# First tokens of the projection: input in four transfers, and two pairs of products taken block by block with the weights' splitting

## The reference

```
x  = L0_attn_x                       # 4 x 1024 x 1024
xn = _layernorm(x, axis=-1)          # (x - mean) / sqrt(var + 1e-5)
q = (xn @ wq.T)                      # 1024 columns: 32 heads of 32
k = (xn @ wk.T)                      # 256 columns: 8 heads
v = (xn @ wv.T)                      # 256 columns
q, k = _apply_rope(q, cos, sin), _apply_rope(k, cos, sin)
...
y = softmax(q k / sqrt(32) + causal mask) v
s = y @ wo.T
g = silu(ffn(xn))                    # a small recurrence on the last token, a gate, a norm
out = x + s * g
```

## Time and profile before

| what | us |
|---|---|
| median of three runs (lowest, highest) | 2590.91 (2590.49, 2593.19) |
| the profiled execution | 2590.74 |
| its span | 2589.1 |
| TensorE busy in it | 2493.8 (96%) |
| VectorE, ACT, POOL busy | 1730.7, 980.8, 1368.0 |

### The profile page before, as it was taken

How to read it: one execution, slowest core, us unless ns; L and a number is a source line. 1 busy time by engine, 2 the same in 40 slices (tenths; PEclk the granted TensorE clock), 3 DMA queues, 4 the chain that set the end, 5 groups by cost and what they waited for, 6 DMA issues and landing times. The chain is left out here.

```text
span 2589.1 us, 43561 instructions
## 1 busy us (share of the span) xinstructions
PE 2493.8 (96%) x14180; PEld 1684.1 (65%) x14180; DVE 1730.7 (67%) x3500; ACT 980.8 (38%) x1645; POOL 1368.0 (53%) x637
## 2 busy tenths in 40 slices
PE   5999999996999999999999999999899999999998
PEld 4888888884555545554455545555378888888886
DVE  6444555444777777777777787777477777777777
ACT  2111111110666655666566656666431111111111
POOL 1122221122999989999899989999711111111111
PEclk9999999997999999999999999999999999999999
DMA  6544444537665665566466556555475666666666
GB/s 243 187 164 151 158 162 176 187 139 240 200 189 164 190 189 166 181 192 206 130 196 194 164 172 199 167 181 183 169 195 108 129 119 120 117 118 119 121 121 122
DMA packets 228017, 428.90 MB, mean 166 GB/s; under 512 B 16836, under 2 KB 99780, under 8 KB 227928
## 3 DMA queue, kind: packets, MB, share of 16 engines
q1 hardware_dynamic: 154536, 375.85, 43.7%
q0 software_dynamic: 73392, 51.91, 13.4%
HBM read 313.67 MB, written 113.51 MB: 165 GB/s over the span
## 5 line engine op out<-in xcount | busy, mean ns | idle before, releaser
L934 DVE CUSTOM_DVE_ANT_0 bcast<-mxp,mask_q 128x128 f32<-128x128 f32 (+7 forms) x1024 | 726.2, 753 | 307.1 <-PE mxp L1041 172.8
L855 ACT ACTIVATE pr<-stp 128x512 f32<-128x512 f32 x1152 | 649.5, 595 | 492.8 <-PE stp L1050 367.7
L1050 PE MATMUL stp<-qs,ks 97*128 97x512 f32 x1152 | 479.0, 454 | 3.5 <-ACT pr L855 2.7
L466 PE MATMUL eo<-xt,w 128*128 128x512 f32 x1920 | 448.8, 393 | 3.6 <-DVE xt L383 3.6
L804 POOL TENSOR_TENSOR acc<-acc,pr 128x2048 f32<-128x2048 f32 x96 | 440.8, 4592 | 4.4 <-POOL acc L804 3.8
L466 PEld LDWEIGHTS eo<-xt,w 128*128 128x128 f32 x1920 | 358.5, 189 | 77.2 <-issue 4.0
L1050 PEld LDWEIGHTS stp<-qs,ks 97*128 97x128 f32 x1152 | 209.4, 189 | 247.1 <-ACT pr L855 116.0
L1419 PE MATMUL gp<-g,xa 128*128 128x512 f32 x1536 | 357.1, 392 | 11.6 <-DVE g L1357 8.2
L1419 PE MATMUL op<-o,ya 128*128 128x512 f32 x1536 | 353.6, 390 | 0.8 <-DVE ya L1407 0.8
L1419 PEld LDWEIGHTS gp<-g,xa 128*128 128x128 f32 x1536 | 290.8, 189 | 72.8 <-DVE g L1357 8.5
L1419 PEld LDWEIGHTS op<-o,ya 128*128 128x128 f32 x1536 | 288.3, 188 | 61.3 <-DVE ya L1407 1.7
(11 more groups left out here) (148 smaller groups left out, 3057.3 us busy)
## 6 DMA issues: line engine op xcount, KB each, us to landing
wch<-in_d_w SPq DMA_DIRECT2D x132, 1024.0 KB, 9.4
qs<-q_scratch SPq DMA_DIRECT2D x192, 256.0 KB, 7.9
xa<-xt_scratch POOLq DMA_DIRECT2D x66, 512.0 KB, 6.1
xt_scratch<-xt SPq DMA_DIRECT2D x16, 2048.0 KB, 14.1
q_scratch<-r SPq DMA_DIRECT2D x64, 512.0 KB, 3.6
yr<-y_scratch POOLq DMA_DIRECT2D x33, 512.0 KB, 5.8
xs<-in_x SPq DMA_DIRECT2D x33, 512.0 KB, 5.5
y_scratch<-ys SPq DMA_DIRECT2D x65, 256.0 KB, 2.1
```

Of the source, the lines that this page charges most:

```text
L466: last = nc.tensor.matmul(out, lhs[a](k), rhs[c](k), start=(k == 0 and (a, c) == (0, 0)), stop=(k == KT - 1 and (a, c) == (1, 0)))
L855: nc.scalar.activation(pr[half][:, :, at:at + P], stp[u % 2][:].rearrange("p (h t) -> p h t", h=REP), ACT.Exp, scale=SCALE).then_inc(act_d ...
L934: last = nc.vector.tensor_tensor_reduce(out=bcast[:, k % 2, hh * step:hh * step + w], in0=mxp[k % 2][:, hh * step + c0:hh * step + c0 + w] ...
L1050: last = nc.tensor.matmul(bank, ks[par][:, j * P:(j + 1) * P], qs[par][:, i // 4, :, (i % 4) * P:(i % 4 + 1) * P], start=True, stop=i != j)
```

## The change

On SP the first half's tokens come in four transfers of 512 KB, each with its own semaphore, and VectorE's statistics of the first half wait for each of them in turn. On TensorE the products of the first two pairs of the first half (`EARLY = 2`) are taken out of the turn: after each block's transposes and splitting come the 12 products of that block for both pairs (2 pairs x 2 output tiles x 3), which sum in the four PSUM tiles over the eight blocks. Both pairs are ready together at the end. In the first half only, the statistics of the second half's tokens come after pair 1 in place of pair 0, the normalising before pair 2 in place of pair 1, and the transposes from the k pair on (table `X_TR_FIRST`). So that the first turn can differ, it is written out ahead of the loop on VectorE, ACT, POOL and TensorE.

```diff
-            sp.dma_start(xin[:], x_block(0)).then_inc(x_in, 16)
+            for tile in range(4):
+                sp.dma_start(xin[:, tile, :], x[tile * P:(tile + 1) * P, :]).then_inc(x_first[tile], 16)
...
                     for q in range(NP):
+                        if q == (1 if first and not half else 0) and not (final and half):
+                            rstd_of(n + 1)
                         pool.wait_ge(r1_done, NP * n + q + 1)
...
-            def statistics(m):
-
-                dve.wait_ge(x_in, 16 * (m + 1))
+            def statistics(m, first=False):
+
+                if not first:
+                    dve.wait_ge(x_in, 16 * m)
                 for t in range(4):
+                    if first:
+                        dve.wait_ge(x_first[t], 16)
                     for c in range(2):
                         last = nc.vector.bn_stats(bst[:, t, c, :], xin[:, t, c * 512:(c + 1) * 512])
...
-                        if q == 1 and not (final and half):
+                        if q == (2 if first and not half else 1) and not (final and half):
                             normalise(n + 1)
...
-                        if q == 0 and not (final and half):
+                        if q == (1 if first and not half else 0) and not (final and half):
                             statistics(n + 1)
...
+            def early_pairs(k):
+                pe.wait_ge(w2_done, k + 1)
+                pe.wait_ge(x2_done, k + 1)
+                for q in range(EARLY):
+                    for e in range(2):
+                        c0 = q * 256 + e * P
+                        for a, c in ((0, 0), (0, 1), (1, 0)):
+                            last = nc.tensor.matmul(eo[q][:, e, :], ws[a][:, k, c0:c0 + P], xt[c][0][:, k, :],
+                                                    start=(k == 0 and (a, c) == (0, 0)),
+                                                    stop=(k == KT - 1 and (a, c) == (1, 0)))
+                    if k == KT - 1:
+                        last.then_inc(pair_done, 1)
+
+            pe.wait_ge(mul_done, EARLY)
             for k in range(KT):
                 transpose_x(0, k, first=True)
-            pe.wait_ge(w2_done, KT)
-            def turn(b, final):
+                if k >= 1:
+                    early_pairs(k - 1)
+            early_pairs(KT - 1)
+
+            def turn(b, final, first=False):
...
                     for q in range(NP):
+                        if first and not half and q < EARLY:
+                            continue
...
-            with pe.Fori(0, B - 1) as b:
+            turn(0, False, True)
+            with pe.Fori(1, B - 1) as b:
                 turn(b, False)
...
+EARLY = 2
+X_TR_FIRST = [[], [], [], [], [0, 1], [2, 3], [4, 5], [6, 7], []]
```

More of the change, by code:

```diff
@@ L199, in project_phase @@
         x_in, stats_done, rstd_done, xn_done = sem("p_x_in"), sem("p_stats"), sem("p_rstd"), sem("p_xn")
+        x_first = [sem(f"p_x_first{i}") for i in range(4)]
         stat_link, issue = sem("p_link"), sem("p_issue")
@@ L327, in turn @@
                     for q in range(NP):
-                        for k in x_tiles(q, final and half):
+                        for k in x_tiles(q, final and half, first and not half):
                             if k == 0 and half == 0:
@@ L342, in turn @@
                                              .rearrange("p (g d) -> p g d", g=KV), ACT.Copy).then_inc(vo_done, 1)
-                        for k in x_tiles(NP + t, final and half):
+                        for k in x_tiles(NP + t, final and half, first and not half):
                             round_x(n + 1, 1 - half, k)
-            with act.Fori(0, B - 1) as b:
+            turn(0, False, True)
+            with act.Fori(1, B - 1) as b:
                 turn(b, False)
@@ L405, in last_tokens @@
                 nc.vector.tensor_tensor(xl, xl, bl, ALU.add).then_inc(xl_done, 1)
-            statistics(0)
+            statistics(0, True)
             normalise(0)
@@ L442, in turn @@
                     for t in range(4):
-                        for k in x_tiles(NP + t, final and half):
+                        for k in x_tiles(NP + t, final and half, first and not half):
                             rest_x(n + 1, 1 - half, k)
-            with dve.Fori(0, B - 1) as b:
+            turn(0, False, True)
+            with dve.Fori(1, B - 1) as b:
                 turn(b, False)
@@ L487, in turn @@
                                 last.then_inc(pair_done, 1)
-                            for k in x_tiles(q, final and half)[e:e + 1]:
+                            for k in x_tiles(q, final and half, first and not half)[e:e + 1]:
                                 transpose_x(n + 1, k)
@@ L509, with x_tiles @@
 X_TR = [[], [], [0, 1], [2, 3], [4, 5], [6], [7], [], []]
-def x_tiles(step, last_block):
-    return [] if last_block else X_TR[step]
+EARLY = 2
+X_TR_FIRST = [[], [], [], [], [0, 1], [2, 3], [4, 5], [6, 7], []]
+def x_tiles(step, last_block, first_block):
+    return [] if last_block else X_TR_FIRST[step] if first_block else X_TR[step]
 def attention_phase(nc, agg_w, agg_b, pn_g, pn_b, d1_w, d1_b, d2_w, d2_b, bc_b, pick,
```

6 lines of the change are left out of this document (2 added, 4 removed).

## The result

| | before | changed |
|---|---|---|
| median, us (lowest to highest, runs) | 2591.91 (2590.49 to 2593.19, 4) | 2566.11 (2565.58 to 2568.36, 4) |
| profiled execution, us | 2590.74 | 2565.86 |
| its span | 2589.1 | 2564.2 |

The ratio is 0.9902, with a 95% interval of 0.9885 to 0.9919. The kernel became 25.8 us faster. (The prediction's 2590.9 was the median of three of the four runs before.)

What follows compares the result with a forecast made beforehand. TensorE was taken to bound the kernel, handing time won in the first half to the end. Terms -3.6, -14.5, +2.9, +1.2, +1.6 make 12.4 us less: 2578.3 from profiled 2590.74, median 2578.5; range 2574.5 to 2584.5.

Steps and rivals of the forecast that it cites:

- Step 1: Start: with four transfers only the last tile's two statistics of eight are left after landing; 3.6 us sooner.
- Step 2: Start: early products sum block by block, 3.20 us a block; both pairs done at 43.4, 18.1 us sooner.
- Step 3: Before pair 2: table `cs` lands at 43.8, VectorE's multiplications wait for it and TensorE stands 2.9 us.
- Steps 4 to 6: TensorE waits 1.2 us before the k pair, 1.6 among v's tiles; pair 0's write lands near 63; normalising takes 5.04.
- Step 7: Written-out turn, the statistics' place, POOL's: no more instructions of work, each waits as before; 0.
- The sum: First half of the tokens: second half's first product at 97.2 against 109.62, 12.4 us less.
- A: Start: the four tiles land together or the statistics gain nothing; 3.6 us less gained, 2582.1; chance 0.13.
- D: Attention's start is set by something else, so the gain is not handed on; 2590.9; chance 0.04.
- E: Start: the clock stays at 1.2 GHz between transposes and waits of each block; 7.9 slower, 2598.8; chance 0.04.
- B: Pair 0's write lands 3 to 5 us after 63, later pairs as late; 2581.5 to 2583.5; chance 0.08.
- C: Before pair 2: TensorE's 2.9 us standing lowers its clock, 3.6 us at half rate lose 1.8; 2580.3; chance 0.05.

Runs made afterwards that it cites:

- e4: The changed kernel with the first tokens in one transfer of 2 MB again; 2569.76 us, ratio 0.9914 to the kernel before.
- e1: The kernel before with only the first 512 tokens in four transfers and the statistics waiting for each; 2586.67 us, ratio 0.9979.
- e7: The changed kernel with the rotation's table `cs` loaded two blocks sooner; 2564.23 us, ratio 0.9898 to the kernel before.
- e5: The kernel before with only 12 one-column memsets more on POOL at its start; 2575.64 us, ratio 0.9944.
- e9: The changed kernel with 244 memsets more on POOL at its start; 2583.11 us, ratio 0.9968 to the kernel before.
- e8: As e7, with the first half's two writes of `xt` moved behind those of pair 1 on SP; 2569.60 us, ratio 0.9919 to the kernel before.
- e6: The kernel before with one-operand reductions in place of VectorE's bias addition and squaring in the attention, so other results; 2573.43 us, ratio 0.9933.
- e2: The kernel before with only the projection's first turn written out on VectorE, ACT, POOL and TensorE; 2580.07 us, ratio 0.9950.
- e3: The kernel before with the projection's first turn written out on POOL alone; 2576.03 us, ratio 0.9939.

## Why the prediction was wrong

- **Step 1 (transfers, -3.6)**: right for the changed kernel, where e4 has 3.65. In the kernel before, e1's trace has 3.7 at the first products and 1.9 at the attention.
- **Step 2 (both pairs done at 43.4; 18.1 us sooner)**: right in its pace (3.19 against 3.20), 1.0 us off in the end (44.4 against 43.4): all 12 products of the first block ran at the lower clock, where I had counted 7.
- **Step 3 (the table, TensorE stands 2.9)**: right, 2.93, and e7 shows that it was the table.
- **Steps 4 to 6 (1.2 and 1.6 us, the write near 63)**: right to 0.2 us in the waits, 1 in the write; that VectorE's normalising takes 5.04 was wrong and cost nothing, since the write was later.
- **Step 7 ("Written-out turn, the statistics' place, POOL's: no more instructions of work, and each waits as before; 0")**: this is the step that failed. It counted what the instructions do and not that there are more of them. Twelve more on POOL are worth 15.5 us in the kernel before (e5), and filling them up to 256 costs 17 us in the changed one (e9). With it failed the sentence "After that the halves repeat as before": true of the projection, not of the attention behind it.
- **The sum**: 11.2 in the start plus e5's 15.5 makes 26.7; measured 25.8. One of the 11.2 is lost on the way to the attention (10.3).
- **The rivals**: A, D and E did not occur. B's write was late by 1 us only, with no cost. C did not occur in the changed kernel, whose clock column stays at 1.00 behind the 3 us without products:

```profile
44.20:47.20 3.00, 0.17 (x1) 1.00 1.05 414
47.40:52.00 4.60, 4.60 (x21) 1.00 0.96 309
```

but did in e8 (behind 3.94 us) and in the trace of e4, where a wait of the same length, 2.90 us, was followed by 3.2 us at half rate, 9 products in place of 16:

```profile
47.80:50.80 3.00, 0.20 (x1) 1.00 1.00 407
...
52.40:55.60 3.20, 3.20 (x9) 0.50 0.97 365
55.80:59.00 3.20, 3.20 (x16) 1.00 1.05 410
```

The range had no case on the fast side but small savings in the start. The rows of the stall were in the trace of before; I read TensorE's gaps of 5 us near 923 only as evidence for the clock, and did not ask what had ended them.

## What to carry to other kernels

A local change has a second effect: it moves all code behind it on each engine that it makes longer (here POOL's counted), and where two engines race for a lock within a few tenths of a microsecond, such a move can decide over several microseconds. When a gain or a loss lies in a phase that the change does not touch, add instructions that do nothing to the kernel before; if they reproduce it, it does not belong to the idea. Here 11 us belong to it, and the other 15 can be had or lost with twelve memsets; they are best made safe by taking the second SBUF operand out of VectorE's operations beside POOL's long ones (e6 shows the worth, 17.7, not a way that computes the same).

## What was not expected of the hardware

- A pause of 0.44 us in a run of POOL memsets with nothing to wait for (e9), and one in the attention (0.45 us idle where 0.14 is usual), both ahead of POOL's 197th record.
- A VectorE addition of 128 x 32 that lasts 4.32 us because it began 0.24 us after a POOL operation, and 0.39 when it began 0.8 us before one.
- TensorE's clock after 3 us without products: kept in the changed kernel (2.93 us), at half rate for 3.2 us in e4 (2.90 us).
- Not settled: why e2 is 4 us slower than e3, with the same two stalls.
